# Attention weights of a vision tower split into fp16 halves by GpSimd's DMAs instead of by ScalarE and VectorE

## What is computed

```python
h = patches @ W_proj.T + b_proj                       # (16, 36, 192)
xn = layernorm(layernorm(h)) * gamma + beta
q, k, v = split(xn @ w_qkv, 3)                        # w_qkv is (192, 2304)
attn = softmax(q @ k.T * 64 ** -0.5)                  # per image and head, 36 x 36
h = h + (attn @ v) @ w_out + b_out                    # w_out is (768, 192)
# then: h += ffn(layernorm(h)) with ternary weights; h += ttt(layernorm(h)); h += moe(layernorm(h))
```

## Time and profile before

| | |
|---|---|
| median of 3 runs | 270.26 us (270.23 to 271.51) |
| profiled execution | 268.91 us, of which the span of the profile is 267.0 us |
| busy share of the span | PE 87%, PE weight loads 68%, DVE 72%, ACT 58%, POOL 44% |
| mean granted TensorE clock | 0.932 |
| DMA queues | POOL's 13.66 MB, SP's 14.60 MB |

### The profile page before, as it was taken

One profiled execution on the slowest core, in us unless ns is written; L12 is line 12 of the kernel. 1 busy time (PEld: TensorE's weight loads), 2 busy tenths in 40 slices (PEclk: granted clock), 3 DMA queues, 4 the chain that ended last, 5 costly groups with the idle time before them and its releaser, 6 DMA issues.

```text
span 267.0 us, 6232 instructions
## 1 busy us (share of the span) xinstructions
PE 233.5 (87%) x2368; PEld 181.4 (68%) x2368; DVE 192.6 (72%) x520; ACT 154.9 (58%) x296; POOL 116.7 (44%) x139
## 2 busy tenths in 40 slices
PE   8979995996696979997988998998999995999991
PEld 3734574785685977453477694885649795999981
DVE  1779999468999579778859869659895434545574
ACT  4679575255579654678489668575361373556510
POOL 9131792011212887375380003403403887866710
PEclk9998999599579797999999999999997997999998
DMA  6998472333800069991017002992390699773262
GB/s 194 305 291 200 120 267 54 72 67 69 275 2 4 5 103 208 210 209 33 1 12 99 0 2 17 139 139 33 35 162 16 121 140 185 104 114 37 27 155 67
DMA packets 25074, 28.66 MB, mean 107 GB/s; under 512 B 11576, under 2 KB 20081, under 8 KB 24949
## 3 DMA queue, kind: packets, MB, share of 16 engines
q0 software_dynamic: 6624, 13.66, 34.0%
q1 hardware_dynamic: 18421, 14.60, 19.6%
HBM read 34.98 MB, written 4.81 MB: 149 GB/s over the span
## 4 chain that ended last, share of the span: by engine, by line
PE 37%; DVE 29%; issue 10%; DMA 9%; ACT 8%; POOL 5%; DVEq 0%; SPq 0%; POOLq 0%; ACTq 0%
DMA y_sum<-arena 4%; PE bank L653 4%; PE bank L523 4%; DMA arena<-x_scratch,arena 3%; DVE arena_k L1034 3%; PE bank L901 3%; PE bank L912 3%; PE bank L536 3%; PE bank L743 2%; PE bank L613 2%; DVE st L965 2%; PE bank L625 2%; POOL arena L1891 2%; PE bank L568 2%; PE bank L720 2%
## 5 line engine op out<-in xcount | busy, mean ns | idle before, releaser
L653 PE MATMUL bank<-tri,idh 128*128 128x512 f16 x148 | 38.5, 380 | 0.0
L1813 POOL TENSOR_TENSOR arena<-arena,ri 128x432 f32<-128x432 f32 x8 | 7.5, 941 | 39.8 <-DVE ri L1083 39.8
L1891 POOL DMA_INDIRECT arena<-x_scratch,arena x14 | 14.8, 1059 | 16.7 <-DVE arena L1447 12.7
L1882 POOL DMA_INDIRECT y_sum<-arena x12 | 18.3, 1522 | 6.9 <-DMA y_sum<-arena 3.1
L1789 POOL TENSOR_TENSOR rs<-arg,mhalf 128x1 f32<-128x1 f32 (+1 forms) x20 | 11.8, 594 | 20.8 <-DVE arg L969 19.4
L653 PEld LDWEIGHTS bank<-tri,idh 128*128 128x128 f16 x148 | 13.7, 98 | 9.7
L584 PE MATMUL bank<-arena,arena_k 96*128 96x288 f16 (+2 forms) x144 | 20.1, 303 | 0.0
L1399 DVE TENSOR_TENSOR arena<-bank,arena 128x360 f32<-128x360 f32 x16 | 8.4, 533 | 15.9 <-PE bank L901 11.7
L613 PE MATMUL bank<-arena_k,arena 128*64 128x72 f16 x288 | 12.7, 220 | 6.5 <-DVE arena L1041 6.5
L584 PEld LDWEIGHTS bank<-arena,arena_k 96*128 96x128 f16 x144 | 14.7, 104 | 4.5
L613 PEld LDWEIGHTS bank<-arena_k,arena 128*64 128x64 f16 x288 | 11.7, 131 | 7.9 <-issue 7.7
(11 more groups left out here) (288 smaller groups left out, 652.7 us busy)
## 6 DMA issues: line engine op xcount, KB each, us to landing
arena_k<-in_w POOLq DMA_DIRECT2D x8, 512.0 KB, 6.3
arena_v<-in_w POOLq DMA_DIRECT2D x8, 512.0 KB, 10.2
arena_v<-in_xT SPq DMA_DIRECT2D x6, 288.0 KB, 4.0
arena_v<-in_wqkv SPq DMA_DIRECT2D x3, 576.0 KB, 7.7
arena_v<-v_scratch SPq DMA_DIRECT2D x32, 54.0 KB
v_scratch<-arena SPq DMA_DIRECT2D x4, 384.0 KB, 2.4
arena_k<-in_w POOLq DMA_DIRECT2D x8, 192.0 KB, 7.0
arena_v<-in_w POOLq DMA_DIRECT2D x8, 192.0 KB, 11.1
```

The costliest lines, as they stand in the source:

```text
L653: mm(bank[IDLE][:, :], idh[:, :], tri[:, 0:1].broadcast_to([128, 512]), start=True, stop=True)
L1882: nc.gpsimd.indirect_dma_start(y_sum[k][:, :], bass.IndirectOffsetOnAxis(ap=sum_at[:, k, e:e + 1], axis=0), ys[:, e, D * k:D * k + D], Non ...
L1891: nc.gpsimd.indirect_dma_start(zr[:, e - 1, XW * k:XW * k + XW], None, x_scr[:, :], bass.IndirectOffsetOnAxis(ap=tok_at[:, k, e:e + 1], ax ...
```

## The change

K and Q weights: POOL issues two DMAs that cast the fp32 original to the high half (after the last block of the input is there), ACT writes the negated high half into the place of the low one, and POOL issues two DMAs that add the original to it. The output weights go the same way: cast after the clearing of `arenaV`, negation on ACT in step 2, addition after the division of pair 2. SP's loads of wk, wq and the output weights go, and DVE's three subtractions. The V weights stay as they were. The clearing of `arenaV` waits for the V weights, for the split of the tokens and, in POOL's order, for ACT's negation of wq.

```diff
@@ sync @@
-            for name, c in (("wv", 2 * AH * AD), ("wk", AH * AD), ("wq", 0)):
-                load(wqkvraw[:, :, c:c + AH * AD], name, d["wqkv"][:, :, c:c + AH * AD])
+            load(wqkvraw[:, :, WV_AT:], "wv", d["wqkv"][:, :, WV_AT:])
...
-            wait_full(sp, "q", HP - 1, 1)
-            load(woraw, "woT")
@@ tensor @@
-                    pe.wait_ge(wqk_lo, 1 if key == "k" else 2)
+                    pe.wait_ge(wk_lo if key == "k" else wq_lo, 16)
...
-                pe.wait_ge(wo_lo, 1)
+                pe.wait_ge(wo_lo, 16)
@@ vector @@
-            for n in range(2):
-                dve.wait_ge(wqk_hi, n + 1)
-                o = slice(768 - 768 * n, 1536 - 768 * n)
-                v.tensor_tensor(wqkv[:, 1, :, o], wqkvraw[:, :, o], wqkv[:, 0, :, o], ALU.subtract).then_inc(wqk_lo, 1)
...
-                if s == PAIRS - 1:
-                    dve.wait_ge(wo_hi, 1)
-                    v.tensor_tensor(woT[:, 1], woraw, woT[:, 0], ALU.subtract).then_inc(wo_lo, 1)
@@ scalar @@
-            a(wqkv[:, 0, :, 768:1536], wqkvraw[:, :, 768:1536], ACT.Copy).then_inc(wqk_hi, 1)
+            a(wqkv[:, 1, :, 768:1536], wqkv[:, 0, :, 768:1536], ACT.Copy, scale=-1.0).then_inc(wqk_negated, 1)
...
-            a(wqkv[:, 0, :, 0:768], wqkvraw[:, :, 0:768], ACT.Copy).then_inc(wqk_hi, 1)
+            a(wqkv[:, 1, :, 0:768], wqkv[:, 0, :, 0:768], ACT.Copy, scale=-1.0).then_inc(wqk_negated, 1)
...
-                if s == 5:
+                if s == 2:
                     act.wait_ge(loaded("woT"), 16)
-                    a(woT[:, 0], woraw, ACT.Copy).then_inc(wo_hi, 1)
+                    a(woT[:, 1], woT[:, 0], ACT.Copy, scale=-1.0).then_inc(wo_negated, 1)
@@ gpsimd @@
+            pool.wait_ge(loaded(f"x{KC - 1}"), 32)
+            for name, c in (("wk", AH * AD), ("wq", 0)):
+                g.dma_start(wqkv[:, 0, :, c:c + AH * AD], d["wqkv"][:, :, c:c + AH * AD]).then_inc(loaded(name), 16)
...
-            pool.wait_ge(wqk_lo, 2)
+            for n, (c, low) in enumerate(((AH * AD, wk_lo), (0, wq_lo))):
+                pool.wait_ge(wqk_negated, n + 1)
+                g.dma_start(wqkv[:, 1, :, c:c + AH * AD], d["wqkv"][:, :, c:c + AH * AD], accum_op=ALU.add).then_inc(low, 16)
             pool.wait_ge(wv_lo, 1)
+            pool.wait_ge(xn_lo, NT)
             wait_full(pool, "embed", NT - 1)
             g.memset(arenaV[0:72, :], 0.0).then_inc(zeroed, 1)
+            g.dma_start(woT[:, 0], d["woT"]).then_inc(loaded("woT"), 16)
...
+                if p == 2:
+                    pool.wait_ge(wo_negated, 1)
+                    g.dma_start(woT[:, 1], d["woT"], accum_op=ALU.add).then_inc(wo_lo, 16)
```

More of the change, by code:

```diff
@@ L37 @@
 MAGIC = 12582912.0
+WV_AT = 2 * AH * AD
 TABLES = ("tri", "iota", "iota8", "slot", "tid", "bmask", "hsel", "bd")
@@ L199, in tower @@
         stage13 = stage_a[0:HF, :].rearrange("p (j n) -> p j n", j=2)
-        woraw = arenaK[:, K_W:K_W + HP * D].rearrange("p (k n) -> p k n", k=HP)
         wiq, w2q = sb("wiq", [HF, 2, 2 * FH], F16), sb("w2q", [128, 4, D], F16)
@@ L255, in tower @@
         negated = sem("expert_hi_negated")
-        x_hi, x_lo, wv_hi, wv_lo, wqk_hi, wqk_lo, wo_hi, wo_lo = (sem(n) for n in (
-            "patch_hi", "patch_lo", "wv_hi", "wv_lo", "wqk_hi", "wqk_lo", "wo_hi", "wo_lo"))
+        x_hi, x_lo, wv_hi, wv_lo, wqk_negated, wo_negated = (sem(n) for n in (
+            "patch_hi", "patch_lo", "wv_hi", "wv_lo", "wqk_high_negated", "wo_high_negated"))
+        wk_lo, wq_lo, wo_lo = (sem(n) for n in ("wk_low_added", "wq_low_added", "wo_low_added"))
         xn_hi, xn_lo, q_hi, k_hi, v_hi, p_hi, p_lo, ao_hi = (sem(n) for n in (
@@ L428, in expert_high @@
                 wait_full(pool, "S", PAIRS - 1)
-                pool.wait_ge(wo_lo, 1)
             if e == E - 1:
```

## The result

The changed kernel is slower: 276.78 us in the median of 4 runs (275.73 to 278.44), against 270.25 (269.97 to 271.51) for the kernel before on the same chip. The ratio is 1.030, with a 95% interval of 1.0242 to 1.0357. The forecast was 268.3, in a range of 265.5 to 271.4, so direction and range were both missed. The profiled execution took 277.20 us with a span of 275.3, which is 8.3 us more than before.

What follows compares the result with a forecast made beforehand. No engine bounds it; DVE's wait for POOL's clearing of arenaV delays the first scores. Gains of 0.6 (clearing), 0.5 (clock), 0.25 and 0.6 (output weights) sum to 1.95 us: forecast 268.3 us, range 265.5 to 271.4.

Steps and rivals of the forecast that it cites:

- If the two streams share evenly: Input loads: wv and POOL's casts share the DMA engines from some 11 us; clearing starts at 27.9, 0.55 us gained.
- the clearing starts at 28.9: 0.45 lost: Worst end for the clearing of arenaV: both casts served before wv, ACT 2.3 us late, 0.45 us lost.
- 0.6 early: Main term: the clearing of arenaV no longer waits for DVE's subtraction; 0.6 us taken, between +1.4 and -0.45.
- L1028 (or its successor) still ends with it: Sign: DVE's short instruction before K and Q's low halves is released when POOL's clearing of arenaV ends.
- The clock: Less PE idling before the first scores ends the lower clock earlier; 0.5 us taken, between 0 and some 2.6.
- The spare: Before PE's Q: wq's addition lands 1.3 us or more before it is needed, plus another 0.5 or so.
- the 7.3 of the sum: Before PE's Q: median time in us from issue to landing of an addition, used to time wq's.
- best case: ACT not late at the negation of wq: the clearing starts at 27.05 instead of 28.45, 1.40 us earlier.
- The output weights' hold: Before the output projection: DVE's L1054 no longer held by POOL, under 0.3 us instead of 0.83; 0.6 us gained.
- the gain of 0.25 + 0.6: Output weights: 0.25 us from ACT's conversion leaving step 5, 0.6 us from POOL no longer holding DVE.
- The rivals: Clock back early, 3 to 5 us gained (0.2); crowded loads, 0 to 1.3 gained (0.28); w_out2 late, slower (0.14).
- Rival 3: Before DVE's L1009: additions and casts delay w_out2, or wq's addition lands late; 271.9 us if w_out2 lands at 33; chance 0.14.

Runs made afterwards that it cites:

- e5: Kernel before, with wk and wq loaded unconverted from POOL's queue instead of SP's; 277.03 us, ratio 1.0300.
- e6: Changed kernel, with SP issuing nothing behind wv until the casts of wk and wq have landed; 272.88 us, ratio 1.0165.
- e7: e6, with the output weights' cast moved from between the clearing and the bias additions to behind those additions; 272.25 us, one run.
- e17: Changed kernel, with only the five bias additions moved behind the division of pair 0; 274.5 us, ratio 1.0189.
- e1: Kernel before, with only the output weights loaded the new way; 269.11 us, ratio 0.9984.
- e10: e6, with the clearing waiting until the additions to wk and wq have landed; 274.31 us, one run.
- e16: e6, with the clearing waiting for DVE's first weight sum; 273.80 us, one run.
- e2: Changed kernel with the output weights as before, so only K and Q go the new way; 277.66 us, ratio 1.0303.
- e3: Changed kernel, with ACT's negation of wk moved behind the five token tiles; 271.47 us, ratio 1.0102.
- e11: e3, with the bias additions moved behind the division of pair 0; 269.33 us, ratio 0.9985.
- e13: e9, with SP's loads of rows put behind those of w_in and w_out2; 266.87 us, ratio 0.9881.
- e9: e6, with the bias additions moved behind the division of pair 0; 268.84 us median, six runs 266.24 to 268.84, five 272.74 to 276.29.

## Why the prediction was wrong

**The step that failed: "If the two streams share evenly ... wv's last 2 us or so take 4 and it lands at about 16.4", and the end that followed, "the clearing starts at 28.9: 0.45 lost".** wv, on SP's queue, wasn't slowed (L1511 at 14.35 against 14.42). wk's cast, which that sum needs by 17.9, landed at 24.4, and wq's at 26.2, 13.5 and 14.5 us after issue. Two things stood in place of an even share from 11 us on. While wv was on its way POOL's queue moved nothing: its first packets come between 14 and 16 us. And after that it did take turns with SP's queue, 180 packets against 173 from 18 to 22 us, but SP's packets were larger (0.65 MB against 0.27), and what it shared with was rows, w_in and w_out2. I took both bounds from who is served first among wv and the casts, and forgot that SP's queue goes on behind wv. "Nothing in the trace shows a queue served first" was true, but then an end of the range has to be the time at which SP's queue has sent what it had issued before. It was there to be worked out: w_out2, the last large load, landed at about 26.4 by my own sum. e5 shows that the lateness belongs to the queue and not to the cast, and e6 that it goes when SP's queue is held (5.1 to 5.9 us). Why POOL's queue moved nothing until wv had landed stays open. The clearing started 5.30 us late instead of 0.6 early.

The rule of the Trainium skill that I weighed (DMA: Bandwidth & Descriptors, Issuing engines are not separate DMA queues) holds in that both queues use the same engines. The same page (Queues, rings and completion order) lets each engine take turns between queues packet by packet. From 18 us on the trace agrees: 180 packets against 173 here, and in e5, from 18 to 22 us, 86 against 81. Equal turns are not equal bytes, though, and for the first 3 us and more behind the issue there were no turns: 288 KB beside SP's full queue took 12.6 us and more, with that queue held at most 6.7 (e7).

**The second step: "L1028 (or its successor) still ends with it [the clearing]".** It was held on to the end of the bias additions behind it, 3.35 us more. By e17 this is 3 us of the loss. The row of before that I generalised was right for a clearing that starts after a wait. The runs sort as follows:

| kernel | clearing stands | bias additions next on POOL (but for a cast) | hold ends with |
|---|---|---|---|
| before, e1, e5, e10, e16 | after a wait | yes | clearing |
| after, e2, e3, e6 | right behind a transfer's issue | yes | bias additions |
| e11, e13, e17 | right behind a transfer's issue | no | clearing |

In these runs the longer hold comes only where both conditions are met. e7 and e9 are not in the table, because DVE reached the instruction after the clearing's end. e1 and e2 exclude the cast, e10 with e16 an addition in flight. How long DVE had been waiting doesn't sort the runs either: at the clearing's end it was 0.9 to 4.3 us in the second row, and 2.3 to 7.8 in the first. Why the issue ahead matters stays open. One thing goes with it: behind it POOL's records overlap by 0.3 to 0.4 us (in the changed kernel the clearing ends at 44.43, the next record starts at 44.04, and the additions at 44.67 before its end at 44.97), where in e1 they follow almost end to start (38.65 and 38.59, 39.37 and 39.39). A POOL that is already in the next instruction might leave DVE no moment to enter; that is only argued. e7 speaks for it, where the additions' records overlap as well and DVE was passed over between them. But e13's records overlap too, with only a transfer's issue behind the clearing, and there DVE got in at 37.57, 0.03 behind the clearing's end; in the changed kernel it didn't, though by the records the additions came only 0.24 us after that end. The Trainium skill (SBUF — State Buffer, Who interferes with whom) has the lock kept for one instruction; in the four kernels of the second row the trace shows DVE passed over at the clearing's end.

**The clock.** Its term (0.5 in the sum) was priced for one idling, that of the first scores. The late casts made a second one, 3.47 us at 27.62, at which PE ran V at 0.50. In the changed kernel this is hidden behind the late clearing, for DVE's chain from its start alone gives the 8.99 us above. In e13, where the first scores start 1.24 us earlier than before and the clock is back a few us earlier, the first softmax sum comes 2.22 earlier: about 1 us for the clock, forecast 0.5. That the shorter idling (2.15 us) brought it isn't shown. The 24 K and Q matmuls behind the first scores took 3.40 us in e13, and 4.75 before and 5.66 in e1, both after 3.28 us of idling; after 4.20 us of it, in e16, they took 3.44. When the clock comes back differs by more than the term between runs with the same idling.

**What held.** In the changed kernel PE's K and Q didn't wait for an addition: they landed 5.3 and 6.2 us after issue, and PE waits between 40 and 60 us for DVE alone. The spare was thin, however. In e3, with the casts late and the clearing early, wq's addition took 8.6 us against the 7.3 of the sum, and PE waited 1.94 us for it; DVE, held to 43.31, still set the end there. With both obstacles gone (e13) the steps can be read as they were meant: the clearing starts at 26.86 (best case 27.05), the first scores at 46.05 (forecast 45.9 to 47.7), and the time is 2.5 us below that of before (forecast 1.95). The output weights' hold went as forecast: 12 elements a partition took 0.83 before and now

```profile
102.65 0.17 DVE L1047 TENSOR_SCALAR b1m<-b1m 108x12 f32<-108x12 f32 x1
```

but the gain of 0.25 + 0.6 that I gave this part can't be told from e1's time (ratio 0.9984, from -0.6% to +0.3%; the gain would be 0.3%), though its last softmax sum is 1.07 us earlier (85.67 against 86.74). Along DVE's softmax sums the changed kernel is 9.26 us late up to the sixth and 8.07 at the eighth: the removed subtraction (1.35) gives back about 1.2.

**The rivals.** None had it. Rival 3 named the right kind (a transfer lands late and everything behind follows one for one), but the wrong transfer: it priced w_out2 and the additions, while wk's cast was late. w_out2 itself was no bound in the changed kernel: the weight sum behind it followed at once on DVE's last low half of x. That sum did start after 30.0 (31.66), which was to be a sign of rival 3, but because the tokens were late. DVE waited for w_out2 in the kernels with SP held and rows ahead of it, 2.3 us (e10) to 5.4 us (e7), and it delayed L1023 past the clearing's end in e7 and e9.

## What to carry to other kernels

Before a load goes to another queue, ask what the old queue still has to send when it is issued: here loads on POOL's queue landed at 24.4 and 26.2 us, and the last load that SP had issued before them at 25.3, so what is needed first must stay ahead in SP's queue, or SP must be held until it has landed. A new queue also reorders what is behind: after holding SP, rows had to go behind w_out2. Where DVE waits out a long POOL instruction, count what stands next on POOL as part of the hold, and put work there that is not urgent elsewhere.

## What the runs showed of the hardware

- 288 KB of fp16 cast by POOL's queue, or 576 KB plain, issued between 10.4 and 13.4 us: 12.6 to 15.1 us to landing beside a full SP queue (after, e2, e3, e5, e11, e17), 4.6 to 6.7 with SP held behind wv (e6, e7, e9, e10, e13, e16). SP's own transfer in progress lost nothing (L1511 at 14.35 against 14.42).
- Once POOL's queue moved, the two queues moved nearly the same number of packets: from 18 to 22 us 180 and 173 (after), 168 and 162 (e3), 86 and 81 (e5), POOL's first. In bytes POOL's had 0.27 MB of 0.92 where it cast (after), and 0.46 of 0.92 where it loaded plainly (e5).
- A DVE operation on 2 elements a partition was held for up to 7.62 us (e3), past the end of the POOL instruction it met, where that one stood right behind a transfer's issue and arithmetic stood behind it. In that order the clearing's record is 10.68 us instead of 10.34, and that of the five additions 3.09 instead of 2.78, but each begins before the record ahead has ended; from that end on they are 10.35 and 2.79.
- e9's runs fall into two groups 4 to 10 us apart. Only one of the upper group is profiled, with w_out2 at 30.9 us; that the lower group had it earlier is likely from e13, where it landed 6.0 us after issue and no run was in the upper group, but wasn't seen.
